# Layer norms by token tile, factor rows by a transfer, key copies in halves, expert weights issued ahead of w2

## The reference

```python
x = x + xattn0(layernorm(x), ctx)   # quantised cross-attention with a feed-forward
x = x + attn0(layernorm(x))         # rotary self-attention, causal
x = x + ffn0(layernorm(x))          # 8 experts whose weights are mixed by a gate, gelu
x = x + xattn1(layernorm(x), ctx)   # 16-head cross-attention over 512 context rows
x = x + attn1(layernorm(x))         # causal self-attention
x = x + ffn1(layernorm(x))          # a linear map by Fourier transform, and a bias
```

## Time and profile before

| | |
|---|---|
| Runs (us) | 375.72, 376.30, 378.17; median 376.3 |
| Profiled execution | 377.07 us, of which the span of the trace is 375.3 |
| Busy in the span | PE 293.2 us (78%), DVE 263.1 (70%), ACT 175.4 (47%), POOL 49.0 (13%) |
| Chain of waits that ended last | PE 56%, DVE 26%, issue 7%, ACT 4%, DMA 4%, the rest under 3% |
| Key copies (L270) | 12 transfers of 512 KB, median 10.4 us from issue to landing |

### The profile page before, as it was taken

One profiled execution on the slowest core, in us unless ns is written; L12 is line 12 of the kernel. 1 busy time (PEld: TensorE's weight loads), 2 busy tenths in 40 slices (PEclk: granted clock), 3 DMA queues, 4 the chain that ended last, 5 costly groups with the idle time before them and its releaser, 6 DMA issues.

```text
span 375.3 us, 7739 instructions
## 1 busy us (share of the span) xinstructions
PE 293.2 (78%) x3040; PEld 179.4 (48%) x3041; DVE 263.1 (70%) x653; ACT 175.4 (47%) x316; POOL 49.0 (13%) x80
## 2 busy tenths in 40 slices
PE   0038484979897996659999996797999999957853
PEld 0013312526453965624445553274666666644742
DVE  3799898957789856658742445696588888675733
ACT  2869495953637644220100000457677777712420
POOL 2041332500000153430002001110000000002001
PEclk9999697989999999659999999687899999995975
DMA  7980000000000699792000000000000000000000
GB/s 178 247 332 1 0 2 0 0 2 3 0 3 1 161 211 218 167 372 79 1 0 1 0 2 0 0 1 2 4 4 3 4 5 3 4 2 0 2 3 29
DMA packets 5357, 19.22 MB, mean 51 GB/s; under 512 B 961, under 2 KB 2113, under 8 KB 4673
## 3 DMA queue, kind: packets, MB, share of 16 engines
q1 hardware_dynamic: 5314, 18.63, 18.1%
HBM read 12.07 MB, written 0.26 MB: 33 GB/s over the span
## 4 chain that ended last, share of the span: by engine, by line
PE 56%; DVE 26%; issue 7%; ACT 4%; DMA 4%; SPq 1%; POOL 1%; POOLq 0%; DVEq 0%; ACTq 0%
PE PS L1057 53%; DVE sm L670 5%; DMA cx<-ctx_in 4%; DVE yq L677 3%; DVE big L730 3%; DVE xn L577 2%; PE PS L1246 1%; DVE yq L739 1%; SPq L253 1%; POOL rstd L297 1%; ACT xT L476 1%; DVE w L833 1%; DVE sm L832 1%; DVE sm L789 1%; ACT sa L368 1%
## 5 line engine op out<-in xcount | busy, mean ns | idle before, releaser
L992 DVE TENSOR_REDUCE sm<-PS 128x1 f32<-128x512 f32 x64 | 43.3, 685 | 11.7 <-PE PS L1057 9.5
L532 ACT ACTIVATE yq<-PS,sm 128x512 f32<-128x512 f32 x44 | 30.1, 687 | 13.9 <-PE PS L1057 13.7
L297 POOL TENSOR_TENSOR rstd<-veps,mhalf 128x4 f32<-128x4 f32 x6 | 6.1, 1018 | 210.1 <-DVE veps L574 210.1
L1057 PE MATMUL PS<-diag,ones 128*128 128x128 f32 x14 | 4.6, 424 | 36.1 <-DVE diag L603 25.6
L1057 PE MATMUL PS<-sa,w 128*32 128x36 f32 (+1 forms) x320 | 30.8, 280 | 2.4 <-ACT w L499 2.4
L368 ACT ACTIVATE big<-PS,cols,sm 128x512 f32<-128x512 f32 (+1 forms) x40 | 32.0, 875 | 0.7 <-PE PS L1057 0.7
L1057 PE MATMUL PS<-yq 128*128 128x384 f32 x96 | 31.1, 486 | 0.0
L476 ACT COPY xT<-PS 128x512 f32<-128x512 f32 x5 | 2.9, 586 | 58.2 <-PE PS L1246 58.1
L1057 PE MATMUL PS<-yq,big 99*128 99x128 f16 x256 | 26.2, 225 | 2.8 <-ACT yq L536 1.5
L1057 PE MATMUL PS<-big,yq 96*128 96x512 f16 x64 | 25.6, 406 | 1.9 <-ACT yq L368 1.9
L1057 PEld LDWEIGHTS PS<-yq,big 99*128 99x128 f16 x256 | 19.4, 100 | 11.9 <-issue 6.7
(11 more groups left out here) (244 smaller groups left out, 627.1 us busy)
## 6 DMA issues: line engine op xcount, KB each, us to landing
big<-yq SPq DMA_DIRECT2D x12, 512.0 KB, 10.4
cx<-ctx_in SPq DMA_DIRECT2D x8, 384.0 KB, 10.8
w<-w_in SPq DMA_DIRECT2D x9, 256.0 KB, 9.5
yq<-w_in SPq DMA_DIRECT2D x1, 2304.0 KB, 8.8
wa<-wa_in SPq DMA_DIRECT2D x1, 1156.0 KB, 18.5
sa<-wx_in SPq DMA_DIRECT2D x1, 768.0 KB, 14.6
rows<-rows_in SPq DMA_DIRECT2D x1, 580.0 KB, 16.2
tern<-rows_in SPq DMA_DIRECT2D x1, 512.0 KB, 4.4
```

Source lines behind the costliest of these rows:

```text
L297: pool.tensor_tensor(rstd[:, :], veps[:, :], mhalf[:, :], ALU.pow).then_inc(s["ln_rstd"], 1)
L532: nc.scalar.activation(pt(i), PS[:, ST_BANK[i % 2], :], ACT.Exp, scale=s1(M_ES))\
L992: V.tensor_reduce(s1(M_MX + i % 8), PS[:, S_BANK[i % 3], :], AX, ALU.max, negate=True)\
L1057: return nc.tensor.matmul(o, lhsT, rhs, start=start, stop=stop, **kw)
```

## The change

Four edits. The norms work by tile in four staggered steps, with 4 variance instructions and 4 powers of one column each. The two memsets of the factor rows are replaced by one memset of a 128 x 128 tile at the start and one DMA with a repeated source, issued behind w2. The key copies are made in two halves of the columns: 24 transfers of half the size, the first 12 once 8 chunks are ready and ahead of the wait for `f2_ps`. The expert loads are issued before the wait for the key copies and the load of w2.

```diff
+        factors = sb("factors", [128, 128])
...
+            def copy_keys(half):
+                c0 = CP // 2 * half
+                sp.wait_ge(s["kp_h"], NCH // 2 * (half + 1))
+                sp.wait_ge(s["kp_l"], NCH // 2 * (half + 1))
+                for r in range(R):
+                    for part in range(3):
+                        sp.dma_start(kst[32 * part:32 * part + 32, r, c0:c0 + CP // 2],
+                                     khl[32 * r:32 * r + 32, part % 2, c0:c0 + CP // 2]).then_inc(s["kst_done"], 16)
+
+            sp.wait_ge(s["pv_ps"], 2 * T)
+            copy_keys(0)
             sp.wait_ge(s["f2_ps"], 1)
             sp.dma_start(tb2, rows_in[:, R_END:R_END + E * D]).then_inc(s["ld_tb2"], 16)
-            sp.wait_ge(s["pv_ps"], 2 * T)
-            sp.wait_ge(s["kp_h"], NCH)
-            sp.wait_ge(s["kp_l"], NCH)
-            for r in range(R):
-                for part in range(3):
-                    sp.dma_start(kst[32 * part:32 * part + 32, r, :],
-                                 khl[32 * r:32 * r + 32, part % 2, :]).then_inc(s["kst_done"], 16)
-            sp.wait_ge(s["kst_done"], 3 * R * 16)
-            sp.dma_start(w2, w2_in.rearrange("p (c e d) -> p c e d", c=FC, e=E1)).then_inc(s["ld_w2"], 16)
+            copy_keys(1)
 
             sp.wait_ge(s["sa_pv"], 1)
             for e in range(1, E1):
                 sp.dma_start(w1[:, e * FF:(e + 1) * FF], w1_in[:, e * FF:(e + 1) * FF]).then_inc(ld_ws[e - 1], 16)
+
+            sp.wait_ge(s["kst_done"], 6 * R * 16)
+            sp.dma_start(w2, w2_in.rearrange("p (c e d) -> p c e d", c=FC, e=E1)).then_inc(s["ld_w2"], 16)
+
+            sp.wait_ge(s["factors"], 1)
+            sp.dma_start(big[96:99, :, :].rearrange("p a (k n) -> p (a k) n", n=128),
+                         factors[96:99, :].unsqueeze(1).broadcast_to([3, 8 * NCH, 128])).then_inc(s["key_ones"], 16)
...
             def rstd_of(n):
-                pool.wait_ge(s["ln_veps"], n + 1)
-                pool.tensor_tensor(rstd[:, :], veps[:, :], mhalf[:, :], ALU.pow).then_inc(s["ln_rstd"], 1)
+                for t in range(T):
+                    pool.wait_ge(s["ln_veps"], T * n + t + 1)
+                    pool.tensor_tensor(rstd[:, t:t + 1], veps[:, t:t + 1], mhalf[:, t:t + 1], ALU.pow)\
+                        .then_inc(s["ln_rstd"], 1)
...
+            pool.memset(factors[:, :], MAX_FACTOR_PAIR).then_inc(s["factors"], 1)
             rstd_of(0)
...
             last_keys_head(0)
-            pool.wait_ge(s["pv_ps"], 2 * T)
-            pool.wait_ge(s["k_evp"], 1)
-            link(pool.memset(big[96:99, 0, :], MAX_FACTOR_PAIR))
             rstd_of(2)
-            pool.wait_ge(s["ln_rstd"], 3)
-            pool.memset(big[96:99, 1, :], MAX_FACTOR_PAIR).then_inc(s["key_ones"], 1)
-            pool.wait_ge(s["key_ones"], 1)
...
+                def tile_stats(t):
                     if product is not None:
+                        dve.wait_ge(s["x_tile"], n_tiles[0] + t + 1)
+                    V.bn_stats(bn[:, t, :], x[:, t, :]).then_inc(s["ln_stats"], 1)
+
+                def tile_moments(t):
+                    if stats:
+                        dve.wait_ge(s["ln_stats"], n_stats[0] + t + 1)
+                    V.bn_aggr(mv[:, t, :], bn[:, t, :]).then_inc(s["ln_mv"], 1)
+
+                def tile_variance(t):
+                    dve.wait_ge(s["ln_mv"], T * n + t + 1)
+                    V.tensor_scalar(veps[:, t:t + 1], mv[:, t, 1:2], LN_EPS, None, ALU.add).then_inc(s["ln_veps"], 1)
+
+                lag = 0 if product is None else 1
+                for i in range(T + lag + 2):
+                    if product is not None and i < T:
                         ps_sem, k = product
+                        dve.wait_ge(ps_sem, T * k + i + 1)
+                        V.tensor_tensor(x[:, i, :], x[:, i, :], PS[:, i, 0:128], ALU.add).then_inc(s["x_tile"], 1)
+                    if stats and 0 <= i - lag < T:
+                        tile_stats(i - lag)
+                    if 0 <= i - lag - 1 < T:
+                        tile_moments(i - lag - 1)
+                    if 0 <= i - lag - 2 < T:
+                        tile_variance(i - lag - 2)
...
                 for t in range(T):
+                    dve.wait_ge(s["ln_rstd"], T * n + t + 1)
                     last = V.tensor_scalar(out_tile[:, t, :], x[:, t, :], mv[:, t, 0:1], rstd[:, t:t + 1],
                                            ALU.subtract, ALU.mult)
...
-            pe.wait_ge(s["kst_done"], 3 * R * 16)
-            pe.wait_ge(s["key_ones"], 1)
+            pe.wait_ge(s["kst_done"], 6 * R * 16)
+            pe.wait_ge(s["key_ones"], 16)
```

More of the change, by code:

```diff
@@ L209, in TW @@
             return tern[:, c:c + n]
-        names = ["ld_x", "ld_id", "ld_cnt", "ld_wf", "ld_ones", "ld_wx", "ld_wa", "ld_w1", "ld_w2", "ld_cst", "ld_cols", "ld_rows", "ld_tb2", "kst_done",
-                 "out_done", "consts", "casts", "wabs", "ws_ps", "ln_veps", "ln_rstd", "ln_out", "gm_diag", "gm_ps",
+        names = ["ld_x", "factors", "ld_id", "ld_cnt", "ld_wf", "ld_ones", "ld_wx", "ld_wa", "ld_w1", "ld_w2", "ld_cst", "ld_cols", "ld_rows", "ld_tb2", "kst_done",
+                 "out_done", "consts", "casts", "wabs", "ws_ps", "ln_stats", "ln_veps", "ln_mv", "ln_rstd", "ln_out", "gm_diag", "gm_ps",
                  "ternary", "txt_q", "txt_tp", "txt_qT", "txt_ps", "fk_tok", "fk_tp", "fkT",
@@ L553, in layer_norm @@
             def layer_norm(n, out_tile, done=None, product=None, stats=True):
-                for t in range(T if stats else 0):
+                def tile_stats(t):
                     if product is not None:
-                        ps_sem, k = product
[L558 to L568, removed]
@@ L569, in layer_norm @@
-                if stats:
-                    link(last)
-                for t in range(T):
[L572 to L576, removed]
+                        dve.wait_ge(s["x_tile"], n_tiles[0] + t + 1)
+                    V.bn_stats(bn[:, t, :], x[:, t, :]).then_inc(s["ln_stats"], 1)
@@ L577, in layer_norm @@
+                if product is not None:
+                    n_tiles[0] += T
+                n_stats[0] += T if stats else 0
+                for t in range(T):
+                    dve.wait_ge(s["ln_rstd"], T * n + t + 1)
                     last = V.tensor_scalar(out_tile[:, t, :], x[:, t, :], mv[:, t, 0:1], rstd[:, t:t + 1],
@@ L582, in layer_norm @@
                     link(last)
-            n_gmax, n_tiles = [0], [0]
+            n_gmax, n_tiles, n_stats = [0], [0], [0]
             def maximum_of(i):
```

## The result

The changed kernel took a median of 366.2 us in its first four runs (361.67 to 366.83) against 376.16 us: ratio 0.9699, 95% interval 0.9613 to 0.9785. Two further series gave 0.9775 (0.9708 to 0.9842) and 0.9673 (0.962 to 0.9726). The ratios leave out runs that are over 1.5% above the fastest of their kernel in a series, which in the third series are four of the changed kernel's eight, and the medians here are of all runs. All 18 runs of the changed kernel have a median of 365.6 us, from 361.7 to 368.7. The 66 runs of the kernel before, in five series, have 375.4, from 370.2 to 378.2; 34 of them ran in two series in which the unaltered changed kernel did not run. The 32 that ran beside the 18 have a median of 374.7 us. So the change is faster by about 9.4 us by the means of these 32 and 18 runs (standard error 0.7) and by 9.1 us by their medians; the forecast was 8.5 us and 367.8 us.

The account below looks back on a forecast made before the run. A POOL memset holding DVE's normalise at norm 2, with the clock lost behind it, bounds the kernel. Terms -5.7 - 0.45 - 2.0 + 0 - 0.4 = -8.6 take 377.07 to 368.5, median 367.8 us; range 365.5 to 371.4.

Parts of the forecast that it names:

- (a): Norm 2: without the two POOL memsets, the transposes begin at about 157.35 instead of 163.08, -5.7 us.
- Rival C: Norm 2: something else, the w2 transfer, holds DVE; no gain but the norms', 376 us; chance 0.03.
- (b): Norm 2's transposes to the first expert product: the clock stays at 1.00, worth -0.45 and -2.0 us.
- Rival A: Behind norm 2: the clock does not hold or rises late, -5.7 us alone, 371.2 us; chance 0.12.
- rival D: Norms 3 to 5: shorter pauses keep the clock up, worth up to 1 us each, 366 us; chance 0.12.
- (c): Key copies in halves, expert weights ahead of w2: not on the path before, weights land in time, 0 us.
- rival B: SP queue: half copies cost as much as whole ones, so expert loads come late, 382 us; chance 0.04.
- The cover theory: Expert weights behind w2: once the stall is gone, PE waits about 4 us for them; gain 2 to 4 us.
- (d): Norms by tile, with one-column variance steps and powers: bounds +0.6 and -1.5 us, the middle taken, -0.4 us.
- collision: In the norms: POOL powers and DVE normalises exclude each other, about 0.2 to 0.25 us more for each of two powers.
- Its own bounds: Forecast time from the terms' bounds: -8.2 -1.5 gives 366.6 us, -7.2 + 0.6 gives 369.7 us.
- the rule cited in the prediction: Factor transfer: spread over the largest number of engines up to 16 dividing its slowest dimension, here 3; term stayed 0.

Follow-up runs that it names:

- Factor rows alone: Kernel before with the two factor-row memsets replaced by the late transfer, nothing else: median 371.5 us against 374.2, ratio 0.9979.
- the memsets elsewhere: Changed kernel with the factor rows written by two POOL memsets behind the wait for the last expert product, no transfer: median 363.7 us, ratio 0.9768.
- the half memset: Changed kernel with three long POOL instructions beside normalises, among them a 3x4096 memset at norm 2: one run, 372.17 us.
- tile norms alone: Kernel before with the tile form of the norms, memsets and queue unchanged: median 374.97 us against 375.96, ratio 1.0001.
- The filler pair: Kernel before and changed kernel, both with seven unread filler products on PE around norms 3 and 4: 373.16 us against 364.44, difference 8.7 us.

## Why the prediction was right in its main steps and wrong in its range

**(a) The stall: -5.7 foreseen.** From norm 2's first addition to the transposes 163.08 - 152.21 = 10.87 us before, 155.09 - 149.99 = 5.10 after: **-5.8**. Not 6.7, because of the context values, as foreseen. Factor rows alone, the memsets elsewhere and the half memset show the cause from three sides. With tile norms alone the held normalise is the one behind the last power, where the memset starts. Rival C (the w2 transfer) has fallen: with the half memset the hold was 3.6 us and ended with the memset.

**(b) The clock: -2.45 foreseen.** From the transposes' start to the first expert product 8.66 before, 161.41 - 155.09 = 6.32 after: **-2.3**. The clock stood at 1.00 at 155 to 157. Rival A did not occur in this trace. Nor did rival D: in both kernels the clock was at 0.50 when the products behind norms 3 and 4 began, and the four halves behind norm 4 took 3.78 us in both.

**(c) The queue: 0 foreseen, 0 measured.** A half copy costs SP 13.67/12 = 1.1 us, half of 26.25/12; rival B needed over 1.9. The weights were issued at 145.94 (148.1 foreseen, less the 2.1 us that the run was ahead). The cover theory, which needed a wait of about 4 us without the queue edits, is shown by the wait of 4.54 us with the factor rows alone.

**(d) The norms: -0.4 foreseen, -0.9 by the traces.** Norm 1, from the first statistics to the rotary products, 3.79 to 3.46 us; norm 3, from the last statistics to the copy, 3.72 to 3.82; norm 4, from the first addition to the copy, 5.12 to 4.81; norm 5 likewise 5.39 to 5.05: -0.33 + 0.10 - 0.31 - 0.34 = **-0.88**. Here two steps failed. The first: I took the middle between a collision of powers with normalises and none. There is none: the powers run at 2.09 us for four, as foreseen, and each normalise at 346 ns inside them. I had carried the hold from two rows with a memset and a multiplication over to a power, a POOL instruction of another kind. Of the POOL instructions that the runs put beside a normalise, the memsets and the tensor_scalar held it and the powers did not; why is not shown. The second: without a collision the prediction had -1.5, which is 0.6 too much. It counted 0.2 us in norms 3, 4 and 5 for transposing hidden on PE, but in norm 4 the time from the end of the last normalise to ACT's copy is 0.56 us before and 0.57 after. The two errors have opposite signs, so the middle was nearer the truth than its reasons. The prediction's own parts for the collision add up to +0.4, not to the bound of +0.6 that it states, which moves the middle by 0.1.

The Trainium skill, SBUF — State Buffer, section on the two separate sides, has the lock, against DVE in a two-port mode, for any GpSimd instruction and its whole length. The trace agrees in the 7.03, 3.61 and 0.76 us and disagrees in the power, where the measurement decides. By the start times here the held normalise is also the earlier of the two (155.85 against 155.87, 363.82 against 363.87), not the later one.

**The sum.** -5.8 - 2.3 - 0.9 is -9.0. The filler pair measures 8.7 to 8.9, the 32 and 18 runs side by side 9.4 with a standard error of 0.7. The forecast had 8.55. So the mechanisms account for the gain within the spread, and term (d), 0.5 us short, is the one that was mis-sized.

**The range.** It failed, and for another reason. The step that failed is "Its own bounds": I built the range from the bounds of my own terms and two rivals, and took the kernel's spread from three runs within 2.5 us. The 66 runs of the kernel before span 8 us and the 18 of the changed one 7. The spread goes with the granted clock: of the 18 runs, the four fastest (361.7 to 362.5 us) have a mean clock of 0.925 to 0.934 and the four slowest (367.5 to 368.7) one of 0.912 to 0.917. The traces show where: it falls in other places in each run, in code that no edit touches, 1.7 us for one set of 32 products, 1.9 us with the other sign in the cross-attention. The prediction had no term for that. 364.8 us, from the ratio of four runs against four, lies 0.7 under the lower end; the ratios of the two further series, on the same 376.16 us, give 367.7 and 363.9. So that the first series fell outside was in part chance, and that the forecast itself lay within 1 us of the gain does not save a range that was too narrow for four runs.

## What to carry to other kernels

A long memset on POOL may cost nothing or nearly its full length, according to what DVE does beside it: look for one instruction of a group whose maximum is far from its median and for the POOL instruction that ends with it. Before a stall is removed, ask what arrives at the end of it: here the expert weights were 4.5 us too late for the new time, and one of two cheap reorderings of the queue sufficed. Where a clock moves the same program by 8 us, take the range from many runs, and size a change only from runs of both kernels in the same series. Fillers on PE narrow the spread, but they need not move two kernels by the same amount, so check in both traces what they did to the clock.

## What the runs showed that was not expected

A power on POOL of 128x16 elements runs for 2.91 us beside a DVE normalise without holding it, where a tensor_scalar of 0.62 us holds one for 0.4 us. DVE's batch statistics run beside a 6.9 us memset in their usual 0.29 us.

The factor transfer is slow: once w2 has landed, the DMA share is 0.15 to 0.17 and the rate 16 to 26 GB/s from 161 to 167, and the transfer goes on until about 169. By the Trainium skill, DMA: Bandwidth & Descriptors, section on why a DMA increments its semaphore by 16, the rule cited in the prediction, it has 3 of 16 engines, which would be a share of 0.19. The trace agrees roughly; with the factor rows alone the share was 0.19, 0.18 and 0.15 from 170 to 176. Nothing waits for the transfer here, but at 16 to 26 GB/s 0.2 MB so laid out would take some 8 to 12 us by itself, an estimate from these rates.

Seven products that nothing reads narrowed the runs of the changed kernel from a spread of 6.8 us to one of 1.2 in one series and 3.2 in the next, and moved its median by under 1 us; they moved the median of the kernel before by 2.2 us.
